# Self attention of the expert block: the queries' parts stored once and repeated by the loads

## The reference

```
def _msa(x, w_qkv, w_proj):
    qkv = (x @ w_qkv).reshape(b, n, 3, H, DK)          # b=4, n=256, H=16, DK=8
    q, k, v = (qkv[:, :, i].transpose(0, 2, 1, 3) for i in range(3))
    attn = softmax(einsum('bhnd,bhmd->bhnm', q, k) / sqrt(DK))
    y = einsum('bhnm,bhmd->bhnd', attn, v)
    return y.transpose(0, 2, 1, 3).reshape(b, n, d) @ w_proj
```

## Time and profile before

| | |
|---|---|
| median of three runs | 2153.54 us (2153.01 to 2155.19) |
| the profiled execution, its own time | 2155.52 us |
| its span, first to last instruction | 2153.7 us |
| mean granted TensorE clock | 0.934 of full speed |
| TensorE matmul busy | 1917.7 us (89%) |
| VectorE busy | 1305.2 us (61%) |
| ScalarE busy | 1291.8 us (60%) |
| the 12 stores of the projection stage, issued | 596.6 to 604.4 us into the span |
| the loads of the first pair of heads, issued | 612.9 to 614.4 us |
| the 32 steps' first scores | 617.9 to 679.9 us |

### The profile page before, as it was taken

One profiled execution on the slowest core, in us unless ns is written; L12 is line 12 of the kernel. 1 busy time (PEld: TensorE's weight loads), 2 busy tenths in 40 slices (PEclk: granted clock), 3 DMA queues, 4 the chain that ended last, 5 costly groups with the idle time before them and its releaser, 6 DMA issues. The chain is left out here.

```text
span 2153.7 us, 43741 instructions
## 1 busy us (share of the span) xinstructions
PE 1917.7 (89%) x17168; PEld 1360.0 (63%) x17168; DVE 1305.2 (61%) x3216; ACT 1291.8 (60%) x2074; POOL 130.7 (6%) x344
## 2 busy tenths in 40 slices
PE   6999999967768559999999999999994699999997
PEld 4677777734634546777777777777772456666663
DVE  6888888876545335554555545555445776666663
ACT  4999999954248115555555555555553356666664
POOL 4000000000022110000000000000000400000000
PEclk9999999977869669999999999999996789999998
DMA  6211111102070520000000000000000621111110
GB/s 230 57 46 44 44 46 45 38 16 70 8 183 2 153 78 1 1 2 1 1 1 1 2 1 1 2 1 2 1 1 11 199 57 47 42 47 46 46 37 17
DMA packets 55291, 87.71 MB, mean 41 GB/s; under 512 B 9865, under 2 KB 31421, under 8 KB 55089
## 3 DMA queue, kind: packets, MB, share of 16 engines
q1 hardware_dynamic: 54577, 83.87, 13.2%
q0 software_dynamic: 512, 1.05, 0.2%
HBM read 66.93 MB, written 17.96 MB: 39 GB/s over the span
## 5 line engine op out<-in xcount | busy, mean ns | idle before, releaser
L2315 ACT ACTIVATE a_prT<-bank 128x512 f32<-128x512 f32 (+1 forms) x448 | 232.7, 565 | 328.0 <-PE bank L2224 327.8
L1110 DVE CUSTOM_DVE_ANT_0 a_attn_junk<-wide,a_mask 128x801 f32<-128x801 f32 (+1 forms) x256 | 247.4, 991 | 123.2 <-PE wide L942 123.0
L1053 ACT ACTIVATE a_attn_prT<-bank 128x512 f32<-128x512 f32 (+1 forms) x448 | 237.0, 566 | 123.0 <-PE bank L959 110.5
L2340 DVE CUSTOM_DVE_ANT_0 a_sc<-wide,a_zeros 128x1024 f32<-128x1024 f32 (+1 forms) x256 | 243.1, 987 | 91.9 <-PE wide L2210 91.9
L1401 DVE CUSTOM_DVE_ANT_0 a_attn_sc<-wide,a_mask 128x801 f32<-128x801 f32 (+1 forms) x256 | 252.8, 988 | 12.0 <-PE wide L1252 10.2
L1268 PE MATMUL bank<-ident,a_attn_sc 128*128 128x128 f32 x1664 | 244.6, 275 | 15.2 <-ACT a_attn_prT L1360 14.1
L1268 PEld LDWEIGHTS bank<-ident,a_attn_sc 128*128 128x128 f32 x1664 | 198.8, 141 | 62.2 <-issue 42.3
L2224 PE MATMUL bank<-ident,a_sc 128*128 128x128 f32 x1664 | 231.3, 277 | 1.5 <-ACT a_prT L2315 1.5
L2224 PEld LDWEIGHTS bank<-ident,a_sc 128*128 128x128 f32 x1664 | 185.4, 141 | 54.4 <-issue 28.1
L2210 PE MATMUL wide<-a_kT,a_qT 64*128 64x512 f32 (+1 forms) x1024 | 211.0, 529 | 0.0
L2276 PEld LDWEIGHTS bank<-a_prT,a_vt 128*64 128x64 f32 x3328 | 180.3, 137 | 48.4 <-issue 47.0
(11 more groups left out here) (448 smaller groups left out, 2537.5 us busy)
## 6 DMA issues: line engine op xcount, KB each, us to landing
a_ks<-a_k_parts SPq DMA_DIRECT2D x384, 75.0 KB
a_k_parts<-a_proj_kp SPq DMA_DIRECT2D x24, 416.0 KB, 4.3
a_qx<-a_q_stack SPq DMA_DIRECT2D x384, 12.0 KB
moe_w1b<-in_e_w SPq DMA_DIRECT2D x15, 256.0 KB, 2.8
ctxT<-in_ctxT SPq DMA_DIRECT2D x4, 832.0 KB, 10.6
a_ctxn<-in_ctxn SPq DMA_DIRECT2D x4, 832.0 KB
m_q_stack<-m_proj_qp SPq DMA_DIRECT2D x9, 256.0 KB, 8.9
m_ks<-m_k_parts SPq DMA_DIRECT2D x24, 96.0 KB
```

The source lines that it names most:

```text
L1053: act.activation(prT[0:keys, u % PRT, kt:kt + m, :], bank_of(s, f"W{g}")[0:keys, 0:m * S].rearrange("p (t q) -> p t q", q=S), ACT.Exp).the ...
L1110: dve.tensor_tensor_reduce(junk[:, n % 2, 0:w], S_WIDE[n % 2][:, 0:w], mask(qt, at, w), 1.0, LOWEST, ALU.add, ALU.max, mx[:, p % 2, qt, e, ...
L2315: copy = lambda out, src: act.activation(out, src, ACT.Copy)
L2340: dve.tensor_tensor_reduce(sc[:, s % 2, h, at:at + w], S_WIDE[h][:, 0:w], zeros[:, 0:w], 1.0, LOWEST, ALU.add, ALU.max, mx[:, s % 2, h, p: ...
```

## The change

The queries' parts are stored once each. The DRAM tensor is laid out by pairs of heads, with a feature's two heads beside one another, so that a pair's row is 2 x 1024 elements (4 KB) in one piece; the columns of the query weights are put into that order on the host. A pair's queries are now loaded in three transfers, one for each part, each of which reads the same 8 rows three times by a stride of zero in front.

```
-def self_project_stage(core, name, w, scale, k_parts, q_stack, vs, pads, load_first):
+def self_project_stage(core, name, w, scale, k_parts, q_parts, vs, pads, load_first):
...
-                for i in range(3):
-                    sp.dma_start(q_stack[:, j, i, :, :], parts["q"][:, j, :]).then_inc(q_stored, 16)
+                sp.dma_start(q_parts[:, j, :, :, :].rearrange("p d h c -> p (d h) c"), parts["q"][:, j, :]).then_inc(q_stored, 16)
...
-            sp.wait_ge(q_stored, 16 * 9)
+            sp.wait_ge(q_stored, 16 * 3)
...
-    q_stack = nc.dram_tensor(name + "_q_stack", (HEADS, 3, 3, 8, B * S), BF16, kind="Internal").ap()
+    q_parts = nc.dram_tensor(name + "_q_parts", (HEADS // 2, 3, 8, 2, B * S), BF16, kind="Internal").ap()
...
-            sp.dma_start(qx[0:STACK, heads, :],
-                         q_stack[heads, :, :, :, :].rearrange("h j i d c -> (j i d) h c")).then_inc(loaded[i], 16)
+            for j in range(3):
+                sp.dma_start(qx[24 * j:24 * (j + 1), heads, :], q_parts[i, j, :, :, :].rearrange("d h c -> d (h c)")
+                             .unsqueeze(0).broadcast_to([3, 8, 2 * B * S])).then_inc(loaded[i], 16)
...
-                    pe.wait_ge(loaded[h // 2], 64)
+                    pe.wait_ge(loaded[h // 2], 96)
...
-    a["m1_w"] = g["L1_ffn_w_qkv"].reshape(D, 3, D)
+    a["m1_w"] = g["L1_ffn_w_qkv"].reshape(D, 3, D).copy()
+    a["m1_w"][:, 0, :] = a["m1_w"][:, 0, :].reshape(D, HEADS // 2, 2, 8).transpose(0, 1, 3, 2).reshape(D, D)
```

More of the change, by code:

```diff
@@ L1729, in load @@
                              k_parts[0, heads, :, :, :].rearrange("h i d c -> (i d) h c")).then_inc(loaded[i], 16)
-            sp.dma_start(qx[0:STACK, heads, :],
-                         q_stack[heads, :, :, :, :].rearrange("h j i d c -> (j i d) h c")).then_inc(loaded[i], 16)
-        self_project_stage(core, name + "_proj", qkv_w, 8.0 ** -0.5, k_parts, q_stack, vs, pads, lambda sp: load(sp, 0))
+            for j in range(3):
+                sp.dma_start(qx[24 * j:24 * (j + 1), heads, :], q_parts[i, j, :, :, :].rearrange("d h c -> d (h c)")
+                             .unsqueeze(0).broadcast_to([3, 8, 2 * B * S])).then_inc(loaded[i], 16)
+        self_project_stage(core, name + "_proj", qkv_w, 8.0 ** -0.5, k_parts, q_parts, vs, pads, lambda sp: load(sp, 0))
         (scored, max_ready, cut, cut_done, rows_ready, rows_in, turned, exp_done, pv_done, u_out, u_turned,
```

## The result

The changed kernel took 2161.55 us (median of 7 runs, 2158.0 to 2165.08), the kernel before 2153.54 (7 runs, 2152.15 to 2155.62): ratio 1.0032, 95% interval 1.0021 to 1.0043. (Ratios are those on record; they are not the quotients of the two medians, which here would be 1.0037.) So the change makes the kernel slower by 5.6 to 7 us, with intervals that reach from 3.4 to 9.3. The forecast was 2155.5, "the same": the direction of its +2 us was right, its size was not. The measurement lies at the end of the range, 2161.0: the median of 2161.55 just above it, the median before times the ratio, 2160.4, just inside.

A forecast was written before the change was run, and what follows sets the result against it. Transfers bound the kernel through step 1's start: stores 2.1 us sooner, slower loads leave pair 1 1.6 late, about 2 with crowding; clock and weights zero. Added to the median 2153.54: 2155.5 us, range 2151.5 to 2161.0.

The forecast's parts named there:

- the same: Whole kernel: 2155.5 us, about 2 us slower, a difference under 0.2% or 4.3 us; chance 66%.
- The number of engines, 3 and 8: DMA: each new query load runs on 3 engines, each new query store on 8, by their outermost counts.
- dividing line of 4.3 us: Start of step 1: from 4.3 us late on, the crowded rival decides; that means 5.2 us for queries a pair.
- crowded rival: Query loads: the three engines go at the crowded rate, step 1 is 7.2 us late, total 2161.5 us; chance 18%.
- The stores: Before SP's start of pair 0: fewer stored pieces on each engine let SP start 2.1 us sooner.
- Start of the queries, issue time: Pair 0's loads: first query data 2.66 us after SP's start; each query load takes SP 0.72 us to issue.
- Pair 0: First pair's loads: there 7.1 us after SP's start, at 617.9 us, where it was at 617.86.
- The step that was too small: Loads of pairs 0 and 1: the next pair's keys running beside the queries add 0.2 to 0.3 us a pair.
- full rate: Query and key loads: 25.6 GB/s an engine for queries, 23.8 for keys, together 4.87 us a pair.
- crowded rate: Query and key loads: 15.5 GB/s an engine, 6.34 us for queries and 1.59 for keys, together 7.93 a pair.
- The clock, "I take zero": Clock rise near 633 us: shifting 2 us against the work would be 0.4 us either way; taken as zero.
- Later pairs: Loads up to pair 7: it lands near 652 us, 17 us before it is wanted at step 25, costing nothing.

The follow-up runs named there:

- e1: Changed kernel with copies placed behind the feature rows, so query loads run on 8 engines and stores on 16: 2154.27 us, ratio 0.9999 to the kernel before.
- e3: Changed kernel with its three query stores laid out to run on 16 engines, loads still on 3: 2157.75 us, ratio 1.0010 to the kernel before.
- e4: Changed kernel with pair 2's loads issued only once pair 1 has landed: 2158.76 us, ratio 1.0017 to the kernel before.
- e2: Changed kernel's loads on 3 engines, but with the nine query-part stores on 16 engines of the kernel before: 2161.61 us, ratio 1.0029.
- e5: Kernel before with a pure delay: the first key part stored twice more and waited for before the loads: 2161.05 us, ratio 1.0032.
- e10: e1 with the four pads issued early, behind the layer norm's transfers: 2146.48 us, ratio 0.9957 to the kernel before.
- e11: Kernel before with the four pads issued early, behind the layer norm's transfers: 2150.27 us, ratio 0.9977.
- e6: e1 with the query loads of pairs 0 and 1 issued by ScalarE's queue instead of SP's: 2154.56 us, ratio 0.9999 to the kernel before.
- e12: Changed kernel with the four pads issued early, behind the layer norm's transfers: 2154.67 us in one run.
- e7: Kernel before with keys stored three times and loaded in one transfer of 72 rows: loads at 211 GB/s; no total time given.
- e8: Kernel before with rows in DRAM 2304 B apart, 2048 B of them used: loads at 191 GB/s; no total time given.

## Why the prediction was right or wrong

- **The number of engines, 3 and 8: right**, to the packet. e1 shows that the number of engines and not the number of transfers makes the loss, e3 prices the stores' 8.
- **The forecast "the same": missed.** A loss of over 0.2% had a chance of 24% in the prediction; the two ratios give 0.26 and 0.32%, and neither interval holds a loss of nothing. Step 1 came 4.55 us late, which by the prediction's own dividing line of 4.3 us is the side of its crowded rival.
- **The stores: right.** 2.1 us forecast, 2.1 measured from the first store (2.3 from the first matmul), and 1.9 more for 16 engines (e3).
- **Start of the queries, issue time: right.** First data at +2.66 forecast, and the trace's first 4 KB piece starts at 612.54, +2.74; SP's query loads took 2.2 us for three.
- **Pair 0: too early by 1.7 us** (+7.1 forecast, 8.8 measured). Two things. The first pieces were slow: 12 GB/s in 612.6 to 613.3 with 2 to 3 engines busy, since the first three took 0.77 to 0.99 us each and not 0.16. Then the keys of pair 1 came by.
- **The step that was too small** is the sentence "As keys of the next pair still run beside them on the other engines, I add 0.2 to 0.3 us a pair". It should have been 1.5. Step 1 came 6.35 us behind step 0; without those keys it is 4.83 (e4), and the forecast's full rate gave 4.87. So the full rate was right for queries alone (80 GB/s at a share of 0.20 in 632.8 to 634.8, 25 an engine), and in 615.6 to 617.2, with keys beside them, 7.7 busy engines (0.48 of 16) moved 113 GB/s, under 15 each. The rival's crowded rate and the forecast's full rate both occur, one after the other. The rival named all queries as slow, and gave 7.2 us for step 1, where it was 4.6.
- **The clock, "I take zero": wrong.** I bounded it by 0.4 us for a rise that moves 2 us against the work, and left out the fall. The rise came 1.9 us later against the work (6.5 against 4.6), and steps 1 to 31 took 0.9 us more, twice the bound. The fall came while the last matmuls were still to run: from step 31 to the last of them it took 19.8 us instead of 17.8 (2.1 before rounding). Together 3.0 us in this profile, two thirds of step 1's own delay. The 14 profiles have both together: where the rise comes 11.9 to 12.4 us behind step 1 (before, e2, e4, e5, e10, e11), steps 1 to 31 take 58.0 to 58.3 us and the fall comes behind the last matmul; where it comes 12.9 to 14.5 us behind (the other eight), they take 58.5 to 59.3 and the fall comes inside the stage.
- **Later pairs: right.** No wait for a transfer behind step 1. The last piece of queries starts at 657.0 us, not 652, still ahead of step 25.
- **The sum.** By the two profiles the stages lose 4.55 + 2.97 = 7.5 us; 0.8 come back ahead of them and 0.7 behind, which leaves the span's 6.0. Neither remainder can be put down to the change: from the last output matmul to the end of the span the 14 profiles take 1453.3 to 1458.6 us, and the changed kernel's two differ by 1.7 (1455.9 and 1454.3). So 7.5 us is the loss in the stages of two profiles, and the ratios' 5.6 and 6.9 us, with their intervals, fit 4.55 as well as 7.5. That the fall inside the stage is what took e1's and e6's gain is read from their profiles (step 31 to last matmul 20.1 in both, 17.8 in the kernel before) and not shown by a run that changes nothing else.

## What to carry to other kernels

Before writing a repeated load, look at its outermost count: here three copies (a stride of zero) in front of 8 rows put it on 3 engines, the same copies behind the rows on 8, and the completion writes in a profile tell which. Bytes saved count only on the engines and at the time where the queue is the longest; here 10 us of padding stood ahead of them. Moving that away gained 5 us by itself (e11), where the change alone lost 6; with it, storing once and loading on 8 engines gained 9 (e10). This stage, which ends in thin TensorE work, took 2 us more or less with where the clock fell, so read step times, not the total, when a change is worth 2 us.

## What the runs showed of the hardware

- The first three 4 KB pieces of the changed kernel's queries took 0.77 to 0.99 us each (12 GB/s in all in 612.6 to 613.3), the ones behind them 0.16 us, 25 GB/s an engine. No run tells why.
- Beside key loads a 4 KB piece of queries took 0.32 us on average (615.6 to 617.2), twice its 0.16.
- From step 31 to the last matmul the stage takes 17.8 us where the clock falls behind the stage (before, e2, e4, e5, e10, e11), 19.8 to 20.2 where it falls some 13 us behind step 31 (changed twice, e1, e3, e6, e12), 21.5 where it falls 6.5 us behind it (e7, e8, where it rises again for a short time before the end). The pattern repeated in two profiles of one kernel.
- In e10 the six stores with an outermost count of 128 took SP 0.32 to 0.46 us each to issue; the changed kernel's six took 0.54 to 0.65. The form alone does not set it: the same form took 0.35 to 0.96 in e2 and e3. A load without a stride of zero took mostly 0.37 us, a query load with one 0.68 to 0.78 in the first three pairs of the changed kernel.
- The loads of both tiles together stay at 186 to 211 GB/s on 12 engines, whatever the pitch in DRAM and with 24 or 72 partitions a transfer, while the stores reach 381 on 16.
